# A graph sum by counting matmuls: float32r one-hots and a weight in two parts in place of bf16 ones and three

## What is computed

```
h  = x @ node_w.T                      # x: 12500 x 64
rf = edge_attr_64 @ review_w.T         # 400000 edges x 64
m  = (h[src] + rf) * edge_weight1      # a row per edge
y  = x + segment_sum(m, dst, 12500)    # dst is sorted
out = (y - mean(y)) / sqrt(var(y) + 1e-5)     # per node, over 64 values
```

## Time and profile before

| | |
|---|---|
| runs, median (range) | 2600.75 us (2598.28 to 2603.38) |
| profiled execution, first to last instruction (its span) | 4402.7 us |
| time of the profiled execution beside its span | none is given |
| TensorE matmul, busy | 2973.6 us, 28844 instructions |
| TensorE weight load, busy | 2163.7 us, beside the matmuls |
| VectorE, busy | 1620.1 us |
| ScalarE, busy | 1200.5 us |
| POOL, busy | 1855.3 us |
| mean granted TensorE clock | 0.791 of full |

### The profile page before, as it was taken

One profiled execution on the slowest core, in us unless ns is written; L12 is line 12 of the kernel. 1 busy time (PEld: TensorE's weight loads), 2 busy tenths in 40 slices (PEclk: granted clock), 3 DMA queues, 4 the chain that ended last, 5 costly groups with the idle time before them and its releaser, 6 DMA issues.

```text
span 4402.7 us, 74924 instructions
## 1 busy us (share of the span) xinstructions
PE 2973.6 (68%) x28844; PEld 2163.7 (49%) x28845; DVE 1620.1 (37%) x4276; ACT 1200.5 (27%) x1951; POOL 1855.3 (42%) x1885
## 2 busy tenths in 40 slices
PE   1767776776766766757777767777567567677676
PEld 1445553555544545535555545455345445455555
DVE  3333332343333333324333333333234333333334
ACT  0222222332222222213222222223223222222223
POOL 5444335434344443453344444443443344444342
PEclk9777787887777787778787777788778777777787
DMA  4121111111111121111111111211111122122111
GB/s 88 41 42 41 40 40 40 40 41 41 41 36 39 39 42 38 40 41 39 40 41 38 40 37 40 42 42 39 39 42 38 35 42 42 36 42 47 34 40 42
DMA packets 491784, 181.43 MB, mean 41 GB/s; under 512 B 449029, under 2 KB 461508, under 8 KB 491206
## 3 DMA queue, kind: packets, MB, share of 16 engines
q1 hardware_dynamic: 259490, 68.52, 7.2%
q0 software_dynamic: 59392, 60.94, 7.2%
q10 hardware_dynamic: 172510, 46.74, 4.9%
HBM read 172.85 MB, written 3.20 MB: 40 GB/s over the span
## 4 chain that ended last, share of the span: by engine, by line
PE 57%; another core or an unknown queue 27%; issue 10%; ACT 4%; DVE 1%; ACTq 1%; DVEq 0%; DMA 0%; SPq 0%; POOL 0%; POOLq 0%
PE count_ps L1235 30%; PE x_sums_ps L1260 18%; ACT counts L1048 4%; PE unit_ps L1166 3%; PE attr_ps L1227 2%; PE turn_ps L1177 1%; PE x_sums_ps L1268 1%; PE turn_ps L1215 1%; DVE hot_lo L747 0%; PE turn_ps L1212 0%; ACTq L1081 0%; PE x_sums_ps L1269 0%; PE attr_ps L1150 0%; DVE hot_key L746 0%
## 5 line engine op out<-in xcount | busy, mean ns | idle before, releaser
L490 POOL DMA_INDIRECT rows<-x,src_cols x1856 | 1845.6, 994 | 2475.0 <-PE unit_ps L1166 1434.0
L1235 PE MATMUL count_ps<-hot_key,hot_lo 128*128 128x343 bf16 x7614 | 1627.5, 366 | 1066.7 <-ACT counts L1048 613.5
L1235 PEld LDWEIGHTS count_ps<-hot_key,hot_lo 128*128 128x128 bf16 x7614 | 799.2, 115 | 1683.7 <-issue 842.1
L1048 ACT ACTIVATE counts<-count_ps 128x686 f32<-128x686 f32 x1269 | 1009.0, 803 | 1752.6 <-remote 947.4
L746 DVE TENSOR_SCALAR hot_key<-count,cols 128x686 bf16<-128x686 f16 x1269 | 531.5, 419 | 2128.6 <-remote 1185.3
L1260 PE MATMUL x_sums_ps<-counts,x_tab 128*64 128x126 f32 (+1 forms) x13916 | 804.6, 275 | 55.9 <-ACT counts L1048 54.8
L1260 PEld LDWEIGHTS x_sums_ps<-counts,x_tab 128*64 128x64 f32 x13916 | 771.2, 139 | 73.3 <-ACT counts L1048 68.8
L747 DVE SCALAR_TENSOR_TENSOR hot_lo<-count,cols 128x384 bf16<-128x384 f16 x1269 | 776.5, 612 | 0.0
L1166 PE MATMUL unit_ps<-rows,unit_hot 128*32 128x128 f32 x3712 | 223.1, 289 | 182.1 <-issue 176.2
L1227 PEld LDWEIGHTS attr_ps<-hot_rel,g_attr 128*128 128x128 f32 x1270 | 257.7, 230 | 94.9 <-issue 59.9
L1166 PEld LDWEIGHTS unit_ps<-rows,unit_hot 128*32 128x32 f32 x3712 | 123.3, 112 | 259.1 <-issue 252.5
(11 more groups left out here) (136 smaller groups left out, 953.1 us busy)
## 6 DMA issues: line engine op xcount, KB each, us to landing
rows<-edge_attr SPq DMA_DIRECT2D x116, 512.0 KB
g_attr<-edge_attr ACTq DMA_DIRECT2D x70, 576.0 KB, 4.6
rows<-x,src_cols POOLq DMA_INDIRECT x1856
out<-x_tab SPq DMA_DIRECT2D x10, 256.0 KB
g_idx<-src ACTq DMA_DIRECT2D x70, 9.0 KB
g_idx<-dst ACTq DMA_DIRECT2D x70, 9.0 KB
g_w<-edge_weight ACTq DMA_DIRECT2D x70, 9.0 KB
stage<-src SPq DMA_DIRECT2D x29, 32.0 KB
```

Of the source, the lines that this page charges most:

```text
L490: pool.indirect_dma_start(out=rows[:, s, t, 0:F], out_offset=None, in_=x, in_offset=bass.IndirectOffsetOnAxis(ap=src_cols[:, c, k:k + 1].b ...
L1048: act.activation(counts[:, :, t * SPAN:(t + 1) * SPAN].rearrange("p (a h) d -> p a h d", a=2), count_ps[t % 2][:, :, 0:HALF].rearrange("p ...
L1235: last = pe.matmul(count_ps[b][:, a, 0:HALF], hot_lo[h][:, i, :], hot_key[h][:, a * HALF:(a + 1) * HALF], start=(i == 0), stop=(i == 2))
```

## The change

Both one-hots become float32r, a four-byte type, and the weight is cut in two: the top part keeps the upper 12 bits of the significand (a mask over the float's lowest 12 bits), the low part is the rest. `hot_lo` has two copies, and a tile is counted with four matmuls. [...] `prepare` has one operation fewer and two waits within in place of three.

```diff
-        hot_key = [sb(f"hot_key{b}", [P, HI * SPAN], BF16) for b in range(HOT_BUFS)]
-        hot_lo = [sb(f"hot_lo{b}", [P, 3, P], BF16) for b in range(HOT_BUFS)]
+        hot_key = [sb(f"hot_key{b}", [P, KEYS], F32R) for b in range(HOT_BUFS)]
+        hot_lo = [sb(f"hot_lo{b}", [P, 2, P], F32R) for b in range(HOT_BUFS)]
...
-        count16 = sb("count16", [P, HI * SPAN], F16)
+        count16 = sb("count16", [P, KEYS], F16)
...
-                dve.tensor_copy(cut[:, 0, :], w_i).then_inc(prep_step, 1)
-                dve.wait_ge(prep_step, 5 * g + 2)
+                dve.tensor_scalar(pack[:, W_TOP, :].bitcast(I32), w_i.bitcast(I32), W_HIGH, None, ALU.bitwise_and
+                                  ).then_inc(prep_step, 1)
+                dve.wait_ge(prep_step, 3 * g + 2)
                 dve.tensor_scalar(pack[:, REL, :], dst_i, tile_first[0:nt, 0:1], None, ALU.subtract)
-                dve.tensor_tensor(pack[:, W1, :], w_i, cut[:, 0, :], ALU.subtract).then_inc(prep_step, 1)
-                dve.wait_ge(prep_step, 5 * g + 3)
-                dve.tensor_copy(cut[:, 1, :], pack[:, W1, :]).then_inc(prep_step, 1)
-
+                dve.tensor_copy(pack[:, LO, :], parts[:, 1, :])
+                dve.tensor_tensor(pack[:, W_LOW, :], w_i, pack[:, W_TOP, :], ALU.subtract).then_inc(prep_step, 1)
+                dve.wait_ge(prep_step, 3 * g + 3)
                 dve.scalar_tensor_tensor(pack[:, KEY, :], parts[:, 0, :], float(SPAN), pack[:, REL, :],
-                                         ALU.mult, ALU.add)
-                dve.tensor_copy(pack[:, LO, :], parts[:, 1, :]).then_inc(prep_step, 1)
-                dve.wait_ge(prep_step, 5 * g + 5)
-                dve.tensor_tensor(pack[:, W2, :], pack[:, W1, :], cut[:, 1, :], ALU.subtract
-                                  ).then_inc(prepared, 1)
+                                         ALU.mult, ALU.add).then_inc(prepared, 1)
...
-                        hot_lo[h][:, :, :], count16[:, 0:P].unsqueeze(1).to_broadcast([P, 3, P]), cols[:, LO, t:t + 1],
-                        cols[:, W1:W0 + 1, t].unsqueeze(2).to_broadcast([P, 3, P]), ALU.is_equal, ALU.mult)
+                        hot_lo[h][:, :, :], count16[:, 0:P].unsqueeze(1).to_broadcast([P, 2, P]), cols[:, LO, t:t + 1],
+                        cols[:, W_LOW:W0, t].unsqueeze(2).to_broadcast([P, 2, P]), ALU.is_equal, ALU.mult)
...
-                    for i in range(3):
+                    for i in range(2):
                         for a in range(2):
-                            last = pe.matmul(count_ps[b][:, a, 0:HALF], hot_lo[h][:, i, :],
-                                             hot_key[h][:, a * HALF:(a + 1) * HALF], start=(i == 0), stop=(i == 2))
+                            last = pe.matmul(count_ps[b][:, a, 0:EVEN], hot_lo[h][:, i, :],
+                                             hot_key[h][:, a * HALF:a * HALF + EVEN], start=(i == 0), stop=(i == 1))
```

More of the change, by code:

```diff
@@ L30 @@
 F16 = mybir.dt.float16
-BF16 = mybir.dt.bfloat16
+F32R = mybir.dt.float32r
 I32 = mybir.dt.int32
@@ L45 @@
 HOT_BUFS = 3
+W_HIGH = -(1 << 12)
 SPAN = 7
@@ L74, in build @@
     HALF = HI * SPAN // 2
+    EVEN = HALF + HALF % 2
+    KEYS = HALF + EVEN
     ROUND_GROUPS = len(STEPS)
@@ L86, in build @@
     assert TILES == PARTS * PER_PART and WIN == 1 << WIN_SHIFT and P == 1 << LO_BITS
-    assert HI % 2 == 0 and HALF <= 512 and HI * SPAN <= 2048 and NS <= P and ALL_CHUNKS <= P
+    assert HI % 2 == 0 and EVEN <= 512 and HI * SPAN <= 2048 and NS <= P and ALL_CHUNKS <= P
     MAX_WINDOWS = (NODES - 1) // WIN + 1
@@ L146, in build @@
         tile_first = sb("tile_first", [GT, 1])
-        w_cut = sb("w_cut", [GT, 2, P], BF16)
-        KEY, LO, REL, W1, W2, W0 = range(6)
+        KEY, LO, REL, W_LOW, W_TOP, W0 = range(6)
         packed = sb("packed", [GT, W0, P])
@@ L534, in _ @@
             pool.memset(fold[:, :], 0.0).then_inc(pool_made, 1)
-            pool.iota(count16[:, :], pattern=[[1, HI * SPAN]], base=0, channel_multiplier=0,
+            pool.iota(count16[:, :], pattern=[[1, KEYS]], base=0, channel_multiplier=0,
                       allow_small_or_imprecise_dtypes=True).then_inc(pool_made, 1)
@@ L718, in prepare @@
                 src_i, dst_i, w_i = g_idx[0:nt, 0, :], g_idx[0:nt, 1, :], g_w[0:nt, :]
-                cut, pack, parts = w_cut[0:nt, :, :], packed[0:nt, :, :], hi_lo[0:nt, :, :]
+                pack, parts = packed[0:nt, :, :], hi_lo[0:nt, :, :]
                 dve.tensor_reduce(tile_first[0:nt, :], dst_i, AX_X, ALU.min).then_inc(prep_step, 1)
```

## The result

The changed kernel takes 2624.73 us (median of 4 runs, 2619.33 to 2629.79), the kernel before 2600.22 us (4 runs): a ratio of 1.0092, with a 95% interval of 1.0081 to 1.0104. It is slower by 24 us, where 145 us less had been forecast, and lies outside the forecast's range (2420 to 2510 us) and outside the wider one (2365 to 2580). In the changed kernel a counting matmul takes 344 columns: the two halves of the 687-column row of hot_key begin at 0 and 343 and share one column.

The account below looks back on a forecast made before the run. TensorE's order was taken to bound the kernel; less 219 us it would end at 2382. POOL's gathers then bound: 2357, plus about 24 and 60.8 behind them, plus 14 for stops, 2456 us; range 2420 to 2510.

Parts of the forecast that it names:

- What bounds the kernel: Whole kernel before the change: TensorE's order sets the end; steps of 33.3 us, together 2590 against a median of 2600.75.
- TensorE's counting: 219 us: Counting matmuls: four float32r in place of six bf16, 0.144 us each, save 3.1 us a step, 219 in all.
- a load is under 0.144 and hidden: Weight loads of the counting matmuls: four-byte loads hide under the matmuls; if bare, up to 0.1 x 4 a tile.
- Rival B: Counting matmuls: float32r streams at the f32 record's pace, 0.30 us a matmul, about 2900 us in all; chance 0.10.
- The loop of two tiles: TensorE and ScalarE's copy through two PSUM buffers: four matmuls of 0.144 plus a fixed 1.17, 1.75 us a pair.
- VectorE: One-hots: hot_key 527 ns, 0.41 us start to start, hot_lo 0.37; 0.78 a tile, 1.56 a pair, covered by TensorE's loop.
- Rival C: One-hots in the counting phase: VectorE becomes the bound at 1.23 us a tile, 2600 to 2690 us; chance 0.08.
- What is late next: POOL: POOL's 1856 gathers at about 1.31 us from start to start become the bound, giving 2456 us in all.
- the present hot_key does not seem to lengthen one: POOL's gathers beside VectorE's hot_key: gathers of 1.50 us are seen where hot_lo runs, not attributed to hot_key.
- rival D: POOL's gathers: the longer hot_key makes all in the counting phase take 1.50, mean 1.38, 2567 us; chance 0.08.
- The end of POOL's chain: Behind unit 112's gathers: its sums and rest of the step, about 24 us, then the tail of 60.8.
- E, the clock: TensorE's counting phase, busy about 1.3 of 1.75 us: the clock falls in part of the steps, 2500 to 2600; chance 0.07.

Follow-up runs that it names:

- b_half: The kernel before with only every second gather of a unit from the fifth unit on: 2601.28 us, ratio 0.9996.
- b_look: The kernel before, unchanged, run once more for a trace without stops: 2600.62 us.
- a_half: The changed kernel with only every second gather of a unit from the fifth unit on: 2451.29 us, ratio 0.9407.
- h16_half: The kernel before remade with two fp16 weight parts and four counting matmuls, with every second gather from the fifth unit on: 2366.49 us, ratio 0.9104.
- a_key16: The changed kernel with hot_key's operation writing 686 bf16 elements to unread tiles, counting matmuls reading float32r zeros: 2482.08 us, ratio 0.9535.
- a_key_short: The changed kernel with hot_key's operation making only the first 344 of its 687 four-byte columns: 2480.72 us, ratio 0.9532.
- h16_long: The fp16 version of the kernel before (four matmuls), with hot_key's 686 columns written twice, 1372 two-byte elements: 2676.83 us, ratio 1.0289.
- h16: The kernel before with the weight in two fp16 parts, both one-hots fp16 and four counting matmuls: 2474.01 us, ratio 0.9507.
- h16_ts: The fp16 version of the kernel before, with hot_lo made by two one-input operations: 2415.46 us, ratio 0.9286.

## Why the prediction was wrong
**What bounds the kernel.** Right. TensorE's order sets the end before the change (b_half: 2601 with half of POOL's work gone), and the step built from stretches without stops, 33.3 us and 2590 in all, was within 11 us.

**TensorE's counting: 219 us.** Mis-sized: 150. The step that failed is "a load is under 0.144 and hidden": a float32r weight load of 128 columns has a mean of 196 ns, a bf16 one 101 (b_look), an fp16 one 102. The prediction read the f32 load's price from matmuls of 14 columns, where the distance of starts was 0.1. A counting matmul costs about 0.17 in place of 0.144. The single records of the traces show where this arises (a_half 1304.2 to 1307.7, h16_half 1331.2 to 1334.6). In a row of float32r matmuls each load starts within 3 ns of the start of the matmul before it and lasts 187 to 192 ns, and the matmuls start 154 to 162 ns apart; of the fp16 ones the load (95 to 100 ns) has ended well before its matmul starts, and the distance is 144 to 150. In a tile that follows a wait or the attr matmuls, the second matmul starts 234 to 266 ns after the first with float32r, 144 to 157 with fp16. Together that is the 0.17 us of a pair on full buffers, 1.54 against 1.37 us. The counting phase of one step, three times three pairs, takes 18.05 us in b_look (1312.38 to 1318.39, 1320.38 to 1326.45, 1327.34 to 1333.31) and 15.88 in a_half (1304.18 to 1309.47, 1311.47 to 1316.82, 1317.70 to 1322.94): 2.17 us a step in place of 3.1, and 70 steps give 152. The Trainium skill (TensorE: Matmul & The Clock Gate, Weight-path perf modes) has fast weight loads for 128 columns of a type other than FP32. By that rule float32r counts as FP32 here: its 196 ns stand beside 193 for the f32 loads of the attr matmuls (a_half). Rival B's bound of 0.30 was far off. How fast the float32r columns themselves stream is not shown apart from the loads; 156 ns for 344 columns is at most 0.45 ns a column.

**The loop of two tiles.** It was put at 1.75 us a pair and takes 1.85 to 1.90. With the counting matmul at 0.168, which is (1.54 - 0.2)/8, the prediction's own loop, four matmuls and the fixed 1.17, gives 1.84: the mechanism was right, and the matmul's size makes most of the difference.

**VectorE.** hot_key was given 527 ns and 0.41 from start to start, and has 586 and 0.49 (1312.68 to 1313.17 below); hot_lo 0.37, and has 0.39. A tile is 0.88 to 0.89, not 0.78, a pair 1.78, still under TensorE's loop of 1.84; a_key16, where the tile is 0.18 us shorter, has the same pairs. So this miss cost nothing on TensorE's chain; what it cost, it cost through POOL. The slope of 0.44 ns an element came from operations of 32 and 128 elements; between 344 and 687 (413 ns in a_key_short, 586) it is 0.50. Rival C, that VectorE alone makes the change worthless, did not come: a_half is 150 us quicker with the same one-hots.

**What is late next: POOL.** Named rightly, and as the forecast's bound. The pace was not. It was put at 1.31, with 1.36 as the bound, as it stood in the kernel before, and there it is right: 1.326 without stops. It became 1.392. The step that failed is the sentence "the present hot_key does not seem to lengthen one" and the 0.08 that rival D got from it. D was the mechanism: a gather that overlaps a hot_key lasts longer, and hot_key is now 0.16 us longer. The timelines of the kernel after, VectorE's and POOL's:

```profile
1312.68 0.57 DVE L745 TENSOR_SCALAR hot_key<-count,cols 128x687 fp32r<-128x687 f16 x1
1313.17 0.48 DVE L746 SCALAR_TENSOR_TENSOR hot_lo<-count,cols 128x256 fp32r<-128x256 f16 x1
1313.56 0.57 DVE L745 TENSOR_SCALAR hot_key<-count,cols 128x687 fp32r<-128x687 f16 x1
1314.05 0.48 DVE L746 SCALAR_TENSOR_TENSOR hot_lo<-count,cols 128x256 fp32r<-128x256 f16 x1
```

```profile
1312.47 0.95 POOL L492 DMA_INDIRECT rows<-x,src_cols  x1 [0.30 <-issue]
1313.72 1.42 POOL L492 DMA_INDIRECT rows<-x,src_cols  x1 [0.30 <-issue]
1315.44 1.13 POOL L492 DMA_INDIRECT rows<-x,src_cols  x1 [0.30 <-issue]
1316.88 1.49 POOL L492 DMA_INDIRECT rows<-x,src_cols  x1 [0.30 <-issue]
```

At 1313.72 and 1316.88 the gathers take 1.42 and 1.49 us. The prediction's long gathers had 1.50 from start to start: here it is 1.72 and 1.79. It read D from one step, in parts of which VectorE stood still, and asked whether the old hot_key lengthened them, when the question was what a longer one would do. D's own pace, with 1.50 in the whole counting phase, was 1.38 and thus nearly met by the 1.392; in it some gathers are longer than D gave and others not held at all. Its time of 2567 fell 50 us short of the span, some 22 by the pace and 28 by the end of the chain, told below. The Trainium skill (GPSIMD Engine Reference, Specifications) names both, VectorE's two-port modes and its instructions with two SBUF inputs, for this contention; the prediction granted only the second half. The runs show operations and not modes, and as far as that goes they agree with both halves: a one-input hot_key moves the gathers by its length (a_key16, h16_long), and the two-input hot_lo holds them more than one-input operations in its place do (h16, h16_ts: 1009 against 977 ns).

**The end of POOL's chain.** The forecast stopped it at the last unit of the steps and added 85 us. The last four units' gathers follow without a pause and only 25 us come behind the last: 9.9 + 1855 x 1.392 + 25.3 against 9.8 + 1792 x 1.392 + 85 = 2589. Some 28 us were lost there; the pace made (1.392 - 1.31) x 1792 = 147. The 14 us that the forecast added for POOL's stops did not come, since POOL no longer waits: 2456 + 147 + 28 - 14 = 2617, the span.

**E, the clock.** It fell to 0.959, together with the waits for rows; with half the gathers, where these are gone, it is 0.988 (a_half). TensorE's chain does not set the end here, so the clock did not cost the gain.

So: of 150 us that TensorE's chain gained nothing arrived. POOL's chain, which would have ended at about 2495 by itself, was made 122 us longer by the same edit (1855 x (1.392 - 1.326)) and ends at 2617, behind the 2599 of the kernel before.

## What to carry to other kernels
Before an edit to the bounding engine is priced, the next chain has to be priced as well, and with the edit in it: an operation that "has cover" on its own engine can lengthen another engine's work. Compare a shorter instruction stream on TensorE with what it does to the operands' makers; here two-byte types gave the same four matmuls, kept hot_key short and the weight loads at 102 ns in place of 196, and turned a loss of 0.9% into a gain of 4.9%, and of 7.1% with hot_lo by one-input operations, for two bits less of the weight. A version with half of the second engine's work, run early, shows within one run how much a change can bring.

## What the runs showed of the hardware
- Float32r counting matmuls of 344 columns, each with its weight load, start 154 to 162 ns apart in an unbroken row (a_half), fp16 ones of 343 columns 144 to 150 (h16_half). A float32r weight load of 128 columns has a mean of 191 to 196 ns, a bf16 or fp16 one of 101 to 102, and 8 matmuls with their two attr matmuls take 1.54 us against 1.37 on full buffers.
- VectorE's one-input operation and POOL's indirect gather get in each other's way. The price depends on how long the operation lasts, or on the bytes that it writes (413 to 416 ns: 1009 to 1013 ns a gather; 580 to 586 ns: 1087 to 1117), and not on its type. The two-input hot_lo costs POOL more than one-input operations that do the same in more time (1009 against 977 ns a gather, VectorE busy 603.0 against 688.8 us).
- Which of the two waits depends on their rhythm: with a VectorE tile of 0.89 us POOL waited, with one of 1.02 us, which stretched to the gather's own 1.25, VectorE did, in three kernels (gathers of 964 to 967 ns, hot_key of 688 to 706). What decides it at the moment that they meet stays open.
